# Two early loads moved from SyncE's queue to ScalarE's

## The reference

```
x = x + layernorm(attention(layernorm(x), W_qkv))
x = x + layernorm(ffn(layernorm(x)))

attention(x): q, k, v = x W_qkv^T in thirds; softmax((q * 128**-0.5) k^T) v, one head, per batch
ffn(x):  h = silu(lin(x, w1) ) * lin(x, w2)      # 128 -> 512
         h = gelu(lin(h, h1)); h = gelu(lin(h, h2))   # 512 -> 512, twice
         lin(h, w3)                                   # 512 -> 128
lin(x, w) = (x w^T) * s      # w ternary (-1, 0, 1), s one scale for each output feature
```

## Time and profile before

| | |
|---|---|
| timed runs, us | 133.56, 133.61, 133.21: median 133.56 |
| span of the profiled execution, first to last instruction | 131.8 us |
| time around the span (median less span) | 1.8 us |
| TensorE busy | 124.8 us, 95% of the span |
| VectorE busy | 106.4 us, 81% |
| ScalarE busy | 97.4 us, 74% |
| GpSimd busy | 28.3 us, 21% |
| moved by the transfers | 8.28 MB, most of it in the first 22 us |

### The profile page before, as it was taken

How to read it: one execution, slowest core, us unless ns; L and a number is a source line. 1 busy time by engine, 2 the same in 40 slices (tenths; PEclk the granted TensorE clock), 3 DMA queues, 4 the chain that set the end, 5 groups by cost and what they waited for, 6 DMA issues and landing times. The chain is left out here.

```text
span 131.8 us, 2374 instructions
## 1 busy us (share of the span) xinstructions
PE 124.8 (95%) x699; PEld 102.7 (78%) x699; DVE 106.4 (81%) x360; ACT 97.4 (74%) x180; POOL 28.3 (21%) x39
## 2 busy tenths in 40 slices
PE   5999998999899999999999999999999999999980
PEld 4676968889886878887879888888776778789970
DVE  1598699999899998938799999566989973996853
ACT  3237878977899919389999277799991996997520
POOL 4263420035200013400200174210002530000351
PEclk9999999999999999999999999999999999999999
DMA  4899996000200000000000001020000002000012
GB/s 110 261 341 384 385 381 198 0 0 5 82 0 5 0 5 2 0 0 0 5 0 0 0 5 40 2 80 7 0 0 0 0 0 84 1 5 0 2 49 76
DMA packets 5344, 8.28 MB, mean 63 GB/s; under 512 B 464, under 2 KB 2768, under 8 KB 5328
## 3 DMA queue, kind: packets, MB, share of 16 engines
q1 hardware_dynamic: 3984, 5.19, 12.0%
q0 software_dynamic: 1344, 2.88, 6.7%
HBM read 7.02 MB, written 1.05 MB: 61 GB/s over the span
## 5 line engine op out<-in xcount | busy, mean ns | idle before, releaser
L317 POOL TENSOR_TENSOR rstd<-ve,minus_half 128x4 f32<-128x4 f32 (+1 forms) x19 | 18.5, 977 | 92.2 <-DVE ve L680 50.4
L1158 PE MATMUL F<-a_hi,h_hi 128*128 128x512 f32 (+1 forms) x160 | 37.6, 357 | 0.0
L1164 PE MATMUL F<-a_lo,h_hi 128*128 128x512 f32 (+1 forms) x160 | 37.3, 353 | 0.1
L612 DVE TENSOR_TENSOR a_lo<-act_full,a_hi 128x512 fp32r<-128x512 f32 (+1 forms) x52 | 30.0, 604 | 3.7 <-ACT act_full L430 3.4
L438 ACT ACTIVATE a_hi<-F,sc 128x512 fp32r<-128x512 f32 (+1 forms) x35 | 21.2, 627 | 14.5 <-PE F L1164 14.4
L1164 PEld LDWEIGHTS F<-a_lo,h_hi 128*128 128x128 f32 x160 | 26.8, 188 | 5.4 <-DVE a_lo L612 1.1
L1158 PEld LDWEIGHTS F<-a_hi,h_hi 128*128 128x128 f32 x160 | 26.0, 188 | 4.4 <-DVE a_hi L718 0.5
L430 ACT ACTIVATE act_full<-F,sc 128x512 f32<-128x512 f32 (+1 forms) x40 | 23.5, 619 | 1.7 <-PE F L1164 1.7
L710 DVE SCALAR_TENSOR_TENSOR act_full<-F,sc,silu 128x512 f32<-128x512 f32 (+1 forms) x16 | 10.7, 681 | 1.7 <-ACT silu L419 1.4
L1115 PE MATMUL F<-x2T_hi,w_hi 128*128 128x512 f32 (+1 forms) x32 | 10.3, 403 | 0.5 <-DVE x2T_lo L612 0.3
L419 ACT ACTIVATE silu<-F,sc 128x512 f32<-128x512 f32 (+1 forms) x16 | 9.8, 635 | 0.9 <-PE F L1118 0.7
(11 more groups left out here) (155 smaller groups left out, 196.9 us busy)
## 6 DMA issues: line engine op xcount, KB each, us to landing
h_raw<-h SPq DMA_DIRECT2D x2, 1024.0 KB, 9.4
h_hi<-h POOLq DMA_DIRECT2D x2, 1024.0 KB, 8.3
xs<-x SPq DMA_DIRECT2D x3, 256.0 KB, 3.9
out<-outs SPq DMA_DIRECT2D x3, 256.0 KB, 2.2
w_raw<-w SPq DMA_DIRECT2D x1, 512.0 KB, 4.7
w_hi<-w POOLq DMA_DIRECT2D x1, 512.0 KB, 7.2
xs<-x SPq DMA_DIRECT2D x2, 128.0 KB, 7.6
w_raw<-w SPq DMA_DIRECT2D x1, 256.0 KB, 12.5
```

The lines of the kernel that those rows point to most:

```text
L317: nc.gpsimd.tensor_tensor(rstd[:, ln, tiles(b)], ve[:, ln, tiles(b)], minus_half[:, 0:SIZES[b]], ALU.pow).then_inc(rstd_ready[ln], 1)
L612: nc.vector.tensor_tensor(dst, full, hi.bitcast(f32), ALU.subtract).then_inc(done, 1)
L1158: nc.tensor.matmul(out, terms[k][0], terms[k][2], start=(k == 0), stop=False)
L1164: last = [nc.tensor.matmul(out, terms[k][0], terms[k][3], start=False, stop=(k == KT - 1)) for out, terms in groups]
```

## The change

Two of SyncE's eleven loads at the head, the x of block 1 and the scales, are taken out of its list and put at the head of ScalarE's program, the scales first. The other nine keep their order on SyncE. Nothing else is altered: the same semaphores count the same transfers.

```diff
@@ SyncE @@
             load_x(0)
             sp.dma_start(wa_raw[:, :], w_attn).then_inc(wa_loaded, 16)
-            load_x(1)
-            sp.dma_start(sc[:, :], scales).then_inc(sc_loaded, 16)
             load_x(2)
             sp.dma_start(w12_raw[:, :], w12).then_inc(w12_loaded, 16)
@@ ScalarE @@
         def _(act):
+            def load_scales():
+                act.dma_start(sc[:, :], scales).then_inc(sc_loaded, 16)
+
+            def load_x(b):
+                act.dma_start(xs[:, tiles(b), :].rearrange("p (g j) d -> p g (j d)", j=2),
+                              x_view[:, G0[b]:G0[b + 1], :]).then_inc(x_loaded[b], 16)
+
@@
+            load_scales()
+            load_x(1)
             qk_copy()
             xT_copy(0)
```

## The result

The changed kernel takes 135.0 us (median of four, 134.56 to 135.44) against 133.44 us: a ratio of 1.01, interval 1.0066 to 1.0134. It is slower, and outside the predicted range of 133.2 to 134.5. The profiled execution took 135.16 us with a span of 133.3, 1.5 us more than before.

The account below looks back on a forecast made before the run. TensorE, busy 100.90 of 102.00 us, bounds the kernel, so only the first block's dependent chain counts. All terms 0 except +0.2 us from late weights: span 131.8 + 0.2 = 132.0, 133.8 us timed; range 133.2 to 134.5.

Parts of the forecast that it names:

- The wait for the scales moves and is worth 0: VectorE's 0.52 us wait before the scales' instruction becomes about 0.48 us before the first scores' maximum; taken as 0.
- SyncE's earlier loads, ScalarE's queue: 0: SyncE's later loads come 0.98 us earlier, unwaited for; ScalarE's issues end 1.5 us before its first copy; both worth 0.
- The weights are late because of the second x: At TensorE's query-key product: the second block's x shares DMA with the attention weights, delaying them by 0.4 us.
- the bound of 0.83: Upper bound in us on the weights' delay: equal shares with the second x, 196.6 kB at 236 GB/s.
- the full-queue rate of 383 GB/s: DMA rate where queues are full, giving 0.51 us of weights' delay; 0.4 us was taken, a little under.
- If that rise stays where it is: First block's transposes on TensorE: starting at 5.93 they meet the faster clock, taking 0.38 us instead of 0.57.
- the late clock at about 135 us: Rival: longer TensorE idle time before the product delays the faster clock, slowing projection and scores by some 1.2 us; chance 0.07.
- The forecast's +0.2 for the wait: Net loss at the first transposes' end: weights 0.4 us late, partly given back by the faster clock; bounds 0 and +0.4.
- All shifts come through: From the first scores into the feed-forward layers no other load is waited for, so all later steps shift equally.
- The colliding issues: Rival: SyncE's and ScalarE's first load issues delay one another, +0.6 to +1.1 us, 134.1 to 134.6 us; chance 0.18.

Follow-up runs that it names:

- e1: Against the kernel before, only the scales' load moved to ScalarE, the second block's x staying on SyncE behind the attention weights: 133.71 against 133.59 us, ratio 1.0001.
- e14: Kernel before, no load moved, with twelve warming matmuls ahead of the query-key product and four behind it instead of ten and six: 133.22 us, ratio 0.9957.
- e5: Kernel before, no load moved, with seven warming matmuls instead of ten ahead of the query-key product: 134.99 us, ratio 1.0123.
- e6: Changed kernel with the query-key product moved behind the first block's transposes and the three warming matmuls after them left out: 133.47 us, ratio 1.0006.
- e8: Against the changed kernel, ScalarE issues the attention weights, then the scales; SyncE issues both first x's: 133.96 us, ratio 1.002.
- e2: Against the kernel before, only the second block's x moved to ScalarE, the scales staying on SyncE: 135.13 us, ratio 1.0114.
- e9: Second profile of the kernel before with seven warming matmuls instead of ten ahead of the query-key product: an execution of 135.27 us.
- e4: Changed kernel with fourteen warming matmuls instead of ten ahead of the query-key product: 133.66 us, ratio 1.0015 to the kernel before.
- e10: Second profile of the changed kernel with fourteen warming matmuls instead of ten ahead of the query-key product: an execution of 134.23 us.
- e13: Changed kernel, both loads on ScalarE, with fourteen warming matmuls ahead of the query-key product and two behind it: 133.47 us, ratio 0.9977 to the kernel before.

## Why the prediction was wrong, point by point

- **The wait for the scales moves and is worth 0**: right. It went, and came back before the maximum, as 2.06 us here and 0.94 us in e1. e14 and e5, with the scales on SyncE, show that it was not even there in every execution of the old order: their profiles have no wait for the scales.
- **SyncE's earlier loads, ScalarE's queue: 0**: right. No new wait for a load but the one named; ScalarE's first copy still follows the product.
- **The weights are late because of the second x**: right in kind, under-sized: 0.4 us taken, 0.70 measured, inside the bound of 0.83. The forecast took the full-queue rate of 383 GB/s; the rows at that time read 236, and in the changed kernel 292 from 2.0 to 4.3 us. By the bound's own working, 196.6 kB at 292 GB/s, that is 0.67 us. In the six traces with the second x beside the weights the product starts at 4.36 to 4.71, in the eight where it is not beside them at 3.61 to 4.12 (e6 and e8 move the product or the weights). The Trainium skill (DMA: Bandwidth & Descriptors, section "Issuing engines are not separate DMA queues") says that such loads interleave on the same DMA engines; e2 and e8 agree, 0.86 us on the weights and 0.75 us on the first x.
- **"If that rise stays where it is"**: this step failed. I let the lateness move the work towards a fixed moment at which the clock rises, and took 0.2 us back. But the lateness also leaves TensorE idle, and the rise then comes later: the matmuls are at 421 ns up to 7.1 us and the projection costs 1.22 us. The moment is not even fixed in kernels without such idle time (5 to 7.8 us over the traces). The mechanism stood among the rivals, as the late clock at about 135 us, with a chance of 0.07 and outside the range; 135.0 was measured. That its figure agrees so closely is in part luck: it was put together from 0.2 us for the wait and 1.2 for the clock, where the start times show 0.70 and 0.82. e5's median and e9's trace show it without any moved load; e4, e10 and e13 show the moved loads without it.
- **How the 1.5 us divide**: not settled. By start times 0.70 us are there at the product and 0.82 arise behind it. With the idle time filled little or nothing is lost in the medians: e4 takes 133.66 against 133.59 us, and e13 133.47 against 133.22 in e14 (the intervals of their ratios overlap). But e13 has two warming matmuls fewer behind the product than e14, which hides part of the lateness, and the traces of slower executions (e13, e10, e4) have the maximum 0.42, 0.55 and 0.94 us later than before. The forecast's +0.2 for the wait lies within this and is not shown. The rest of the loss goes with the idle time.
- **All shifts come through**: right, 1.52 us at the maximum, 1.5 us of span, and so in fourteen traces.
- **The colliding issues**: wrong as a rival. The first x is issued in 0.38 us and lands after 2.2 us, with ScalarE's issue beside it. The Trainium skill (Perfetto Trace Analysis, section "DMA Instruction — HWDGE (DVE, Sync)") speaks of an exclusive lock; no row here shows a wait for it: the scales' issue took 0.40 us on ScalarE against 0.47 on SyncE before, the second x's 0.46 against 0.43.

Open: what decides, from one execution to the next, whether the faster level comes early. The kernel before has executions from 133.06 to 134.63 us on one chip and one of 135.25 and one of 135.85 on two others, and a profile holds only one.

## What to carry to other kernels

Before a load is moved to a second queue, list what is in flight with it in the first microseconds: a load asked for later than its neighbour should not travel beside it. Count TensorE's idle time ahead of the first real matmul as a cost of its own: here three matmuls on zeros fewer, which left 0.61 us of idle time in one trace and 1.12 in another, cost 1.3 us in the median. Two such matmuls, moved from behind the product to ahead of it, gained 0.4%, while no new place of a load gained anything. When a step of a forecast holds a moment fixed, such as the rise of the clock, ask what the change does to that moment.

## What was not expected of the hardware

- The faster level of TensorE's clock came between 9 and 10 us in the four traces in which TensorE idled 0.72 to 1.38 us ahead of its first real matmul, and between 5 and 7.8 us in the twelve others. With the same loads, three warming matmuls fewer made a median of 134.99 instead of 133.66 us, and 1.38 us of idle time cost no more than 0.72.
- The same program's attention weights reached TensorE at 3.61 us in one execution and at 4.12 in another.
- A load of 256 KB needed 3.7 us when issued at 1.17 and 7.5 us when issued at 2.93 on the same queue, behind another queue's megabytes.
